# First edge stage of a graph network: gathers written out on GpSimd, six slots of rows given back by TensorE

## The reference

```
h   = maximum(layernorm(x), 0)
e   = relu(edge_attr_64 @ ee_w1 + ee_b1) @ ee_w2 + ee_b2     # self edges added with attribute 0
msg = h[src] + e
agg = segment_sum(msg, dst)
y   = MLP of three matmuls with two layernorms over (1 + eps) * h + agg
x   = x + relu(layernorm(h + y))
```

## Time and profile before

| | us |
|---|---|
| median of 3 runs | 3407.08 (3405.07 to 3407.32) |
| profiled execution: its own time | 3410.1 |
| profiled execution: span from first to last instruction | 3408.2 |
| TensorE busy | 2566.7 (75%) |
| VectorE busy | 2285.9 (67%) |
| ScalarE busy | 1454.7 (43%) |
| GpSimd busy | 1992.3 (58%) |

### The profile page before, as it was taken

One profiled execution on the slowest core, in us unless ns is written; L12 is line 12 of the kernel. 1 busy time (PEld: TensorE's weight loads), 2 busy tenths in 40 slices (PEclk: granted clock), 3 DMA queues, 4 the chain that ended last, 5 costly groups with the idle time before them and its releaser, 6 DMA issues. The chain is left out here.

```text
span 3408.2 us, 97011 instructions
## 1 busy us (share of the span) xinstructions
PE 2566.7 (75%) x33058; PEld 2437.6 (72%) x33059; DVE 2285.9 (67%) x4707; ACT 1454.7 (43%) x3683; POOL 1992.3 (58%) x2153
## 2 busy tenths in 40 slices
PE   0577777777677758999999999994777777777773
PEld 0567666677676658999999999984776766776762
DVE  8677777777766744666666666665776766766676
ACT  5334434443333436777777777772111111111110
POOL 3666667776666633334443333333777777777774
PEclk9978888888887869999999999996888888888786
DMA  5545555554444420000000000002555655555554
GB/s 137 155 138 148 145 143 150 151 151 137 141 140 133 137 75 9 19 18 18 18 18 18 19 19 18 18 19 90 170 175 172 174 169 172 173 171 174 169 176 117
DMA packets 185718, 374.52 MB, mean 110 GB/s; under 512 B 43924, under 2 KB 95514, under 8 KB 185598
## 3 DMA queue, kind: packets, MB, share of 16 engines
q0 software_dynamic: 75552, 209.66, 22.1%
q1 hardware_dynamic: 107954, 162.91, 15.8%
q10 hardware_dynamic: 2092, 0.74, 0.1%
HBM read 347.36 MB, written 25.80 MB: 109 GB/s over the span
## 5 line engine op out<-in xcount | busy, mean ns | idle before, releaser
L450 POOL DMA_INDIRECT rows<-tab_scratch,idx x784 | 763.0, 973 | 355.9 <-issue 221.2
L1451 POOL DMA_INDIRECT a_rows<-tab_scratch,a_srcs x784 | 749.3, 956 | 240.9 <-issue 233.3
L1518 PE MATMUL sum_ps<-feat,a_hot 128*125 128x132 f32 x3920 | 609.0, 321 | 237.2 <-DVE feat L1611 124.6
L1518 PEld LDWEIGHTS sum_ps<-feat,a_hot 128*125 128x125 f32 x3920 | 565.9, 225 | 255.6 <-DVE feat L1611 135.7
L905 PE MATMUL z_ps<-ah,w 128*128 128x125 f16 x6400 | 554.9, 219 | 2.7 <-PEq L981 0.6
L905 PE MATMUL z_ps<-al,w 128*128 128x125 f16 x3200 | 543.8, 218 | 0.0
L905 PEld LDWEIGHTS z_ps<-ah,w 128*128 128x128 f16 x6400 | 490.5, 97 | 7.4 <-issue 7.3
L515 PE MATMUL sum_ps<-rows,hot 128*125 128x128 f16 x1960 | 370.5, 241 | 126.0 <-PEq L548 118.4
L505 PE MATMUL mlp_ps<-ewa,eab 128*128 128x128 f16 x1576 | 235.0, 238 | 284.2 <-PEq L500 283.1
L1461 ACT ACTIVATE feat<-d 128x32 f32<-128x32 f32 x196 | 45.0, 229 | 827.5 <-DVE d L1607 578.8
L482 ACT ACTIVATE rh<-mlp_ps 128x1024 f16<-128x1024 f32 x196 | 199.2, 1016 | 448.8 <-ACTq L481 420.5
(11 more groups left out here) (208 smaller groups left out, 5985.8 us busy)
## 6 DMA issues: line engine op xcount, KB each, us to landing
ea<-edge_t SPq DMA_DIRECT2D x394, 128.0 KB
dstb<-dst_flat SPq DMA_DIRECT2D x98, 512.0 KB
rows<-tab_scratch,idx POOLq DMA_INDIRECT x784
a_rows<-tab_scratch,a_srcs POOLq DMA_INDIRECT x784
tab_scratch<-prow SPq DMA_DIRECT2D x50, 128.9 KB
hx<-x SPq DMA_DIRECT2D x50, 125.0 KB
x_scratch<-x SPq DMA_DIRECT2D x50, 125.0 KB
hs<-tab_scratch SPq DMA_DIRECT2D x50, 125.0 KB
```

Source lines behind the costliest of these rows:

```text
L450: pool.indirect_dma_start(rows[:, s, k, :], None, dram["tab0"], bass.IndirectOffsetOnAxis(ap=idx[:, s, k:k + 1], axis=0),).then_inc(rows_r ...
L1451: pool.indirect_dma_start(rows[:, b % DEEP, k, :], None, dram["tab1"], bass.IndirectOffsetOnAxis(ap=srcs[:, c:c + 1], axis=0),).then_inc(r ...
L1518: ins = pe.matmul(out[:, c], hot[:, h, k, :], feat[:, row, k, c], start=(k == 0 and c is NARROW[0]), stop=(k == CB - 1 and c is NARROW[-1] ...
```

## The change

- GpSimd: the loop is gone. All 784 gathers of the stage are written out, each reading its indices straight from `srcs`. From batch 6 on GpSimd waits for `rows_free` itself, against a constant that grows by one a batch.
- `rows` has six slots (DEEP) instead of four, `idx` and `idx_ready` are gone. `srcs` lies in the memory of `st`, a tensor that only the next stage writes.
- TensorE: its loop takes six batches in a pass (32 passes) and four batches behind it are written out, so the table is read 33 times instead of 49, six numbers at a time.
- VectorE: `advance` no longer waits for `rows_free` and no longer copies indices. The four index copies ahead of the stage are gone. The ten place-holding increments of `lines` become four.

```diff
-        idx = m.sb("idx", [P, RING, CB], I32)
-        rows = m.sb("rows", [P, RING, CB, 2 * D], F16)
+        srcs = sb["st"][:].rearrange("p t c -> p (t c)").bitcast(I32)
+        DEEP = 6
+        FULL, REST = divmod(NB, DEEP)
+        rows = m.sb("rows", [P, DEEP, CB, 2 * D], F16)
...
         @block.gpsimd
-            with pool.Fori(0, NB // RING):
-                for s in range(RING):
-                    pool.wait_ge(idx_ready[s], 1)
-                    pool.sem_inc(idx_ready[s], -1)
-                    for k in range(CB):
-                        pool.indirect_dma_start(
-                            rows[:, s, k, :], None, dram["tab0"],
-                            bass.IndirectOffsetOnAxis(ap=idx[:, s, k:k + 1], axis=0),
-                        ).then_inc(rows_ready[s], 16)
+            pool.wait_ge(ld_idx, 16)
+            for b in range(NB):
+                if b >= DEEP:
+                    pool.wait_ge(rows_free, b - DEEP + 1)
+                for k in range(CB):
+                    c = CB * b + k
+                    pool.indirect_dma_start(
+                        rows[:, b % DEEP, k, :], None, dram["tab0"],
+                        bass.IndirectOffsetOnAxis(ap=srcs[:, c:c + 1], axis=0),
+                    ).then_inc(rows_ready[b % DEEP], 16)
...
         @block.tensor
-            with pe.Fori(0, NB // RING) as i:
-                tiles = tiles_of(nc, PE, table, RING * i, RING)
-                for u in range(RING):
+            with pe.Fori(0, FULL) as i:
+                tiles = tiles_of(nc, PE, table, DEEP * i, DEEP)
+                for u in range(DEEP):
+                    body(tiles, i, u)
+            tiles = tiles_of(nc, PE, table, DEEP * FULL, REST)
+            for u in range(REST):
+                body(tiles, FULL, u)
...
         @block.vector
-            def indices(b, s):
-                dve.tensor_copy(idx[:, s, :], srcs[:, bass.ds(CB * b, CB)]).then_inc(idx_ready[s], 1)
...
-                dve.wait_ge(rows_free, 1)
-                dve.sem_inc(rows_free, -1)
-                indices(b - 1 + RING, ring)
...
-            dve.wait_ge(ld_idx, 16)
-            for b in range(RING):
-                indices(b, b)
...
-            for _ in range(10):
+            for _ in range(4):
                 dve.sem_inc(lines, 1)
```

More of the change, by code:

```diff
@@ L346, in edges0 @@
         acc, iota16, negbase, ewa, ewb = sb["acc"], sb["iota16"], sb["negbase"], sb["ewa"], sb["ewb"]
-        srcs = m.sb("srcs", [P, NCH], I32)
+        srcs = sb["st"][:].rearrange("p t c -> p (t c)").bitcast(I32)
+        assert NT * 2 * HEADS == NCH
         dsts = m.sb("dsts", [P, NCH + CB], F32)
-        idx = m.sb("idx", [P, RING, CB], I32)
+        DEEP = 6
+        FULL, REST = divmod(NB, DEEP)
         table = m.sb("table0", [1, 2, NBP + 4], I32)
-        rows = m.sb("rows", [P, RING, CB, 2 * D], F16)
+        rows = m.sb("rows", [P, DEEP, CB, 2 * D], F16)
         ea = m.sb("ea", [P, 2, BE], F32)
@@ L372, in edges0 @@
         ld_tab = m.sem("ld_tab")
-        idx_ready = [m.sem(f"idx_ready{s}") for s in range(RING)]
-        rows_ready = [m.sem(f"rows_ready{s}") for s in range(RING)]
+        rows_ready = [m.sem(f"rows_ready{s}") for s in range(DEEP)]
         ea_ready = [m.sem(f"ea_ready{s}") for s in range(2)]
@@ L406, in _ @@
         def _(sp):
-            sp.dma_start(srcs[:], t["src_cols"]).then_inc(ld_idx, 16)
+            sp.dma_start(srcs, t["src_cols"]).then_inc(ld_idx, 16)
             sp.dma_start(table[:, :, 0:NBP + 1], dram["sched"][:, 0:NBP + 1].unsqueeze(0)).then_inc(ld_tab, 16)
@@ new lines, in body @@
+            def body(tiles, i, u):
+                s = u % 2
+                edge_mlp(1 - s)
+                lo, end = tiles[u]
+                pe.wait_ge(hot_ready, 1)
+                pe.sem_inc(hot_ready, -1)
+                pe.wait_ge(sum_free, 1)
+                pe.sem_inc(sum_free, -1)
+                pe.wait_ge(r_split, 1)
+                pe.sem_inc(r_split, -1)
+                pe.wait_ge(rows_ready[u], 16 * CB * (i + 1))
+                sums(sum_ps[:, s, :], s, u, s).then_inc(sum_done, 1)
+                with pe.If(end > lo + 1):
+                    with pe.Fori(lo + 1, end):
+                        pe.wait_ge(xhot_ready, 1)
+                        pe.sem_inc(xhot_ready, -1)
+                        sums(sum_ps[:, 2, :], 2, u, s).then_inc(xsum_done, 1)
+                pe.matmul(used_ps[:], ewa[:, 0:1], ewa[:, 0:1], start=True, stop=True).then_inc(r_free, 1)
+                pe.matmul(used_ps[:], ewa[:, 0:1], ewa[:, 0:1], start=True, stop=True).then_inc(rows_free, 1)
@@ L568, in add @@
                 dve.tensor_tensor(a, a, sum_ps[:, s, :], ALU.add).then_inc(sum_free, 1)
-            def main_hot(b, row, lo):
-                one_hot16(dve, hot[:, row], iota16, dsts, negbase, b, lo)
             def extra_hot(b, x):
@@ L596, in low_activations, with advance @@
                                          op0=ALU.max, op1=ALU.subtract).then_inc(r_split, 1)
-            def advance(b, s, ring, lo, end, following):
+            def advance(b, s, lo, end, following):
                 with dve.If(end > lo + 1):
@@ L641, in turn @@
                     if u or not isinstance(i, int):
-                        advance(b, s, (u - 1) % RING, *tiles[u], tiles[u + 2][0])
+                        advance(b, s, *tiles[u], tiles[u + 2][0])
                     else:
```

## The result

The changed kernel takes 3387.62 us (median of 5 runs, 3379.97 to 3391.78) against 3407.08 for the kernel before: a ratio of 0.9946, 95% interval 0.9934 to 0.9957. It is about 19 us faster; 69 were forecast, and 3388 lies outside the stated range of 3303 to 3380. The profiled execution took 3391.64 us, with a span of 3389.8.

The account below looks back on a forecast made before the run. No engine was full: a ring of engines waiting for each other, with VectorE's instruction fetches the main removable loss. -48.8 - 12 - 3 - 5 = -68.8 us gave 3338 us against the median; range 3303 to 3380.

Parts of the forecast that it names:

- The stall, -48.8: VectorE's wait before its reduction while its loop's program is fetched again; the change would end it, saving 48.8 us.
- 26 us of clock: Possible extra gain from TensorE's slower matmuls behind weight passes, 2.4 us a pass over 11; the forecast took 0.
- four packets of 8 KB with one fetched ahead: VectorE's program store: four packets stay, a fifth drives out the first; the changed loop needs three and one ahead.
- the reading by which the stall would stay: Two 16 KB lines with a third fetched ahead: VectorE's loop would lose its first line again, about 3387 us.
- Index copies and start, -12 and -3: VectorE's index copies gone, -12 us (bounds 0 and -34); GpSimd's first gather earlier, -3 us (bounds 0 and -5).
- TensorE's passes, -5 between -28 and +28: Fewer TensorE table-load stops, 33 instead of 49, against stops no longer shared with VectorE: -5 us taken.
- count of stops: With passes of six against four, both engines stop together at 17 batches, TensorE alone at 16, VectorE alone at 32.
- Slots, waits, gathers: Six slots, GpSimd's own wait for free rows and written-out gathers on GpSimd were costed at nothing extra.
- The stall stays: Rival, chance 0.12: VectorE's program is still fetched at each jump, only 20 us come, 3387 us.
- the second rival: Chance 0.08: GpSimd's gathers become the bound, ending no earlier than 1104 us; gain capped near 116 us, 3291 us.
- TensorE's loop is not fetched anew: Third rival, chance 0.07, claimed the opposite: TensorE's longer loop is refetched in 33 passes, 145 us on top, 3483 us.
- None of the four: Signs: 40 us idle before reduction; recurring 16 KB TensorE packets; sums awaiting gathers; split-edge-attribute waits grown over 28 us.

Follow-up runs that it names:

- f1: The kernel before with twelve place-holders in place of ten, VectorE's outer loop at 448 to 725: 3347.9 us, 0.9838 of before.
- f2: The changed kernel with twenty place-holders in place of four, VectorE's outer loop at 446 to 712: 3442.9 us, 1.0105 of before.
- f3: The changed kernel with DEEP = 4: TensorE passes of four batches, four slots, loads of four numbers: 3331.2 us, 0.9781 of before.
- f4: The changed kernel with TensorE's six numbers read as eight from an aligned table of their own: 3306.4 us, 0.9700 of before.
- g8: f3 with TensorE's loads reading eight numbers from an aligned start, four of them used: 3305.4 us, 0.9716 of before.
- g6: The changed kernel with four slots, a TensorE pass of eight batches and loads of twelve aligned numbers: 3312.5 us, 0.9736 of before.
- g9: The changed kernel with six slots, a TensorE pass of twelve batches and loads of sixteen aligned numbers: 3376.4 us, 0.9919 of before.
- g5: f3 with TensorE loading six numbers from an unaligned start, four of them used: 3385.2 us, 0.9950 of before.

## Why the prediction was wrong

- **The stall, -48.8: right.** The fetches ended, and 55 us came (f1, 46 to 64), 54 went when they were brought back (f2). The forecast had put 26 us of clock behind the weight passes and taken 0 of it; some of it may have come, since TensorE is busy 16 us less in f1's trace. Of the places: 446 to 723 and 446 to 712 are fetched, 448 to 725 and 430 to 696 are not. That is what the forecast's four packets of 8 KB with one fetched ahead give. Two lines of 16 KB, as the Trainium skill has it ("Runtime: NRT & Kernel Launch", section "Instruction fetch mechanics"), would give the same four answers if they began at 448 and 704 and nothing were fetched ahead. But here three lines would be six packets of 8 KB and come in pairs, where the trace has five a weight pass, one at a time. The runs rule out only the reading by which the stall would stay.
- **Index copies and start, -12 and -3: right in their sum, not shown apart.** 19 us (9 to 30) by f3 against f1, together with whatever the gathers' form brings. The start's 3 did not show: the gathers begin 3.6 us earlier, but the first sums 0.2 us later than before.
- **TensorE's passes, -5 between -28 and +28: this step failed.** It measured +56 (the changed kernel against f3). "VectorE's take 0.81 each, for six numbers" was carried over to TensorE's six, and the bound above was made of stops at the old 1.76 us, so it couldn't hold a longer one. What the two rows differed in was neither engine nor count: VectorE's loads begin at entry 4i of the table, TensorE's at 4i + 1, and in the changed kernel at 6i + 1. A load that begins there pays for every number. With 1.467 us a load the two loads of a stop became 2.9 us, against VectorE's 1.6, and the slower clock behind it came on top (0.86 against f4's 0.91). The forecast's count of stops (16 of TensorE alone) was sound; what such a stop is worth no run shows, as f4 and g8 are both held by the gathers.
- **Slots, waits, gathers: right.** A gather takes 972 ns against 973, and only three sums waited for rows, 2.7 us together.
- **The sum.** -55 - 19 + 56 = -18, which is the result's 0.9946. It must come out, since f1 and f3 are steps on the way from before to the changed kernel; what they tell is the share of each step. The forecast's first three terms were -63.8 and came as -74; the fourth was wrong by 61.
- **The rivals.** "The stall stays" gave 3387 and the time is 3388. That is chance: the stall went, and another loss of its size came. The gathers did not become the bound of the changed kernel, but they did in f4, g8 and g6: the second rival's mechanism and its pace (784 gathers in 998 us; 995 in f4) were right, and it only needed shorter loads. In f4 the last gather begins at 1116 us, against the 1104 that the rival gave as the earliest end; the 17.7 us that GpSimd still waits cover the difference. (By the rival's own numbers, 1223 less 1104, its cap is 119 us and not 116.) TensorE's loop is not fetched anew at six batches, but is at twelve (g9).
- **The signs of being wrong.** None of the four appeared, and the forecast failed all the same. The one that was meant for TensorE's passes, waits for the split edge attributes grown by more than 28 us, was set against the kernel before, whose 155.5 us held the stall. The fair comparison is f1: 122.2 us there against 138.6 in the changed kernel from 200 to 1100 us.
- The change with passes of four would have been 3331 us, with aligned loads 3306. Best are f4 and g8, 3% below before; g8 needs only one line more than f3.

## What to carry to other kernels

Price a moved or resized operation from a row with the same operands and the same start, not from the row of the same count; if two rows for the same operation differ, find out in what before choosing between them. A short stop of the engine that all wait for can cost more than its length, since its clock falls too: 46 us of longer loads cost 58 (f3 to g5). When several variants come out at the same time, look whether another engine has run out of waits before concluding that what they differ in is worth nothing. A change that undoes one loss and makes another of the same size looks like a change that did nothing: look at the rows of each step, not at the sum.

## What the runs showed of the hardware

- A table load into registers from a start that is a multiple of four numbers takes 0.59 us for eight, 0.85 for twelve, 1.11 for sixteen (TensorE), and 0.60 for eight, 0.81 for six (VectorE): about 0.26 us for each four more. From the other starts seen (one, two or three numbers beyond such a multiple), four take 1.00 us and six 1.47 (TensorE; 1.43 on VectorE): about 0.24 us for each number. Eight numbers can cost less than half of six.
- VectorE's loop of weight passes is fetched anew, in five packets of 8 KB, at each jump back at 446 to 723 and not at 448 to 725: 55 us for two instructions' difference in place.
- TensorE's loop of some 1,410 instructions stays, one of some 2,110 is fetched in ten packets of 16 KB a pass, for 4.3 us at each jump back.
- 784 gathers written out take 995 us of GpSimd (f4), 0.975 us each with 0.3 us between them; this is the floor of the stage once TensorE's and VectorE's stops are short.
